# Two attentions of a fused kernel: the softmax division moved from PE transposes and DVE to a DMA round trip and GpSimd, with a new order of PE work in the causal attention's slots

## The chip, the cores and the metric

One core of a Trainium2 chip. The metric is the device time of one run in microseconds, a median over the runs shown; smaller is better.

## The reference, cut to what matters

Two layers over 16 batches of 512 tokens and 128 features. Layer 0 adds to x the output of a memory module that is trained on the sequence, and of a block made of a convolution, full attention (16 heads of size 8) and a dense mixture of 8 experts. Layer 1 adds causal attention, run twice: the second pass takes its queries from a convolution over the first pass's context, with the same keys and values. It also adds a mixture with 32 experts and top-8 routing.

```python
# layer 0
x = conv1d(x); q, k, v = split(x @ wqkv.T + bqkv)          # 16 heads of 8
ctx = softmax(q @ k.T / sqrt(8)) @ v
# layer 1
ctx = causal(q, k, v)                                      # "first" turn
q2 = conv1d(ctx) + conv_b
ctx2 = causal(q2, k, v)                                    # "second" turn
out = ctx2 @ out_w.T + out_b
```

## The kernel before

It has four stages, one after the other: `learn`, `attend0` (the attention of layer 0; tiles named `c_...`), `mixture` (`a_...`) and `layer1` (both causal attentions and the routed experts; `b_...`, `r_...`). The change touches only `attend0` and `layer1`, which share the class `Attention`.

**Turns and slots.** An attention of one batch is a turn. `attend0` has 16 turns. `layer1` has 32: `turns` mixes first passes and second passes as f0, f1, f2, s0, f3, s1 and so on. A turn has 16 slots: slot s is group g = s // 4 (four heads) and key tile t = s % 4. I call the slots t = 0 to 3 of one group a quarter. In slot s, turn p's scores for this tile are made (`tensor_scores`, L1286, and in the causal case the mask products of L1293), the exponentials are taken on ACT (`b_prob`, `c_prob`, L1401), and the product with the values of an earlier slot is added to the accumulator in bank 7 (`tensor_values`, L1317). Beside it PE makes the scores of turn p+1 in the other layout (L1254, masks L1260) for DVE to take row maxima (L1461). The maxima are transposed (L1267), split in two on DVE (L1469, L1470: `shift`) and written into turn p+1's query rows by DMA (L1232, `sync_shift`).

In the causal case the widths shrink: scores are 512, 384, 256 and 128 wide for t = 0 to 3. For t = 0 and 1 the four heads come in two units of two heads, `scores(0)` and `scores(1)`; for t = 2 and 3 they are one unit.

**Two PSUM rings set the order.** `s` has three banks of 512 columns (scores for the exponentials, convolution, queries, keys, the `whole` transposes); `m` has two pairs of banks (maxima, shift, context, values, output). PE runs its instructions in the written order. When it wants a bank that ACT or DVE has not yet freed, everything behind waits.

**The context.** An accumulation lasts two groups, a pair: two pairs a turn. After it ACT copies the accumulator to `c` (L1407, `scalar_context`, in slot 8 for pair 0 and in slot 0 of the next turn for pair 1); each head has 8 rows of sums and a ninth row, the softmax denominator. PE transposes `c` (`tensor_context`, L1327, four transposes, slots 9 and 1), DVE takes the reciprocal of the denominators and multiplies (`vector_context`, L1481, L1483), into `ctxn`. In slot 3 PE transposes both halves back (`tensor_whole`, L1335) and ACT copies them: in `attend0` to `ctxt` (L1780), which is stored to memory (L1655); in `layer1` to `cpad` for a first turn, the input of the convolution (L2894), or to `ctxt` (L2935) for a second turn, the input of the output projection (L2913).

**Other work in the turns.** In `layer1`, in the turn two ahead of a first pass: queries in slot 0 (L2885), keys in slot 4 (L2889), values in slot 8 (L2905). Two ahead of a second pass: the convolution in two halves in slots `CONVOLVE` = (4, 8). The output projection stands in slot `OUTPUT` = 5 of the turn behind a second pass. After keys or convolution GpSimd splits the queries (and keys) into three bf16 parts (`pool_parts`, L1181 to L1187), and SP spreads them to rows with 6 or 12 DMAs (`sync_rows`, L1208, L1211). SP's queue in a turn of `layer1` is, in order: `sync_shift(p, 1)`, expert weights, a load of the sums, `sync_rows(p + 2)`, a load of x (L1912), `sync_shift(p + 1, 0)` (slot 12), and the store of a result. The queue of GpSimd is: bias of a result (L2865), gathers, `pool_parts(p + 2)`, scatter-adds. Turns 0 to 8 of `layer1` also carry the routed experts.

## Time and profile before

| | |
|---|---|
| median of 3 runs | 3461.34 us (3455.52 to 3463.75) |
| the profiled execution: its time, and its span | 3481.77 us, 3480.0 us |
| mean granted TensorE clock of the profiled execution | 0.969 |
| busy share of the span | PE 92%, PE weight load 54%, DVE 74%, ACT 60%, GpSimd 24% |
| `attend0` | its context copies run from 448.8 to 1144.7 us |
| `layer1` | its context copies run from 2296.6 to 3470.4 us |

The span is the profiled execution seen by the trace; what lies around it is 1.8 us. The profiled execution took 20 us more than the median of the runs, so differences are carried over, not totals. Busy time of PE is modelled: matmuls overlap, and the start of one to the start of the next says more than a duration.

### The profile page before, as it was taken

To read this page: it belongs to the slowest core of one execution; us is meant where nothing else is said; L and a number is where in the kernel's file an instruction comes from. 1 tells how busy PE (TensorE), PEld (TensorE's weight loads), DVE (VectorE), ACT (ScalarE), POOL (GpSimd) and SP (SyncE) were. 2 spreads that over 40 slices of the span, in tenths; PEclk is the share of its full clock that TensorE was granted. 3 is DMA by queue.
4 is the path that set the end of the run, shared out by engine and by line. 5 is a ranking of instruction groups with operands and counts; after the bars stand their busy time and mean duration, and the time that the engine had idled before them with its cause. 6 is when DMAs were issued, how large, how long until landed. Compare 5 with 4: busy or idle time off the path is not lost. (4 is left out here: it accounts for less than half of the span.)

```text
span 3480.0 us, 80944 instructions
## 1 busy us (share of the span) xinstructions
PE 3216.7 (92%) x32139; PEld 1880.7 (54%) x32139; DVE 2559.9 (74%) x5088; ACT 2087.3 (60%) x4201; POOL 831.7 (24%) x756
## 2 busy tenths in 40 slices
PE   6887599999999899999999999789999999999998
PEld 5876233333333577777777777545555545444454
DVE  5876788888887376667667667677777777777774
ACT  6774188888888443434343434156667777776766
POOL 3321111111110242242242243223332211111110
PEclk8998799999999999999999999789999999999998
DMA  4100211111110001011011001222222121112110
GB/s 140 33 13 1 62 47 56 56 56 56 56 43 28 27 23 36 23 33 36 23 33 30 29 23 33 64 60 62 59 60 42 53 61 45 48 42 57 39 32 25
DMA packets 180487, 152.11 MB, mean 44 GB/s; under 512 B 44388, under 2 KB 160900, under 8 KB 179972
## 3 DMA queue, kind: packets, MB, share of 16 engines
q1 hardware_dynamic: 173092, 141.21, 14.4%
q0 software_dynamic: 6144, 4.72, 1.0%
q8 instruction: 271, 4.44, 0.5%
q10 hardware_dynamic: 864, 0.79, 0.1%
q14 instruction: 116, 0.95, 0.1%
HBM read 48.45 MB, written 32.65 MB: 23 GB/s over the span
## 5 line engine op out<-in xcount | busy, mean ns | idle before, releaser
L1461 DVE TENSOR_REDUCE b_maxima<-psum 128x2 f32<-128x1024 f32 (+3 forms) x768 | 774.4, 1045 | 239.0 <-PE psum L1260 215.3
L1401 ACT ACTIVATE b_prob<-psum 128x512 f32<-128x512 f32 (+2 forms) x1536 | 725.6, 526 | 329.0 <-PE psum L1293 299.9
L1461 DVE TENSOR_REDUCE c_maxima<-psum 128x2 f32<-128x1024 f32 x512 | 594.3, 1219 | 60.4 <-PE psum L1254 60.3
L1401 ACT ACTIVATE c_prob<-psum 128x512 f32<-128x512 f32 x1024 | 551.1, 597 | 121.6 <-PE psum L1286 101.2
L2213 PEld LDWEIGHTS psum<-consts_layer,a_hid 128*128 128x128 f32 x4096 | 476.2, 192 | 53.6 <-issue 53.3
L2203 PE MATMUL psum<-a_x1t,consts_layer 128*128 128x512 f32 x1024 | 464.0, 599 | 16.1 <-issue 10.5
L2213 PE MATMUL psum<-consts_layer,a_hid 128*128 128x128 f32 x4096 | 477.8, 274 | 0.0
L2273 ACT ACTIVATE a_hid<-psum,consts_layer 128x512 f32<-128x512 f32 x512 | 348.1, 687 | 211.0 <-PE psum L2203 205.1
L1286 PE MATMUL psum<-b_qa,b_ka 64*128 64x512 bf16 (+3 forms) x2048 | 365.5, 303 | 60.8 <-ACT b_prob L1401 56.5
L1317 PE MATMUL psum<-b_prob,b_v 128*32 128x512 f32 (+3 forms) x4096 | 387.6, 451 | 0.2
L2435 DVE SCALAR_TENSOR_TENSOR a_acc<-psum,a_gprob,a_acc 128x128 f32<-128x128 f32 x512 | 143.7, 343 | 270.4 <-PE psum L2213 258.4
L1317 PE MATMUL psum<-c_prob,c_v 128*32 128x256 f32 (+1 forms) x3840 | 320.2, 405 | 1.6 <-ACT c_prob L1401 0.6
L1254 PE MATMUL psum<-b_ka,b_qa 62*128 62x512 bf16 (+3 forms) x2048 | 300.2, 307 | 20.5 <-DVE b_maxima L1461 11.7
L2203 PEld LDWEIGHTS psum<-a_x1t,consts_layer 128*128 128x128 f32 x1024 | 188.1, 192 | 220.9 <-issue 210.9
L1286 PEld LDWEIGHTS psum<-b_qa,b_ka 64*128 64x128 bf16 x2048 | 123.2, 93 | 298.0 <-ACT b_prob L1401 221.7
L1293 PE MATMUL psum<-b_kmask,b_pick 64*128 64x64 bf16 x4096 | 253.0, 191 | 0.0
L1254 PE MATMUL psum<-c_ka,c_qa 62*128 62x512 bf16 x1024 | 202.9, 388 | 33.2 <-DVE c_maxima L1461 17.9
L1260 PE MATMUL psum<-b_qmask,b_pick 64*128 64x64 bf16 x4096 | 221.9, 191 | 2.5 <-issue 2.5
L1260 PEld LDWEIGHTS psum<-b_qmask,b_pick 64*128 64x128 bf16 x4096 | 194.7, 97 | 52.7 <-issue 5.8
L1293 PEld LDWEIGHTS psum<-b_kmask,b_pick 64*128 64x128 bf16 x4096 | 185.2, 95 | 46.9 <-issue 1.1
L1286 PE MATMUL psum<-c_qa,c_ka 64*128 64x512 bf16 x1024 | 205.9, 387 | 0.9 <-ACT c_prob L1401 0.8
L1254 PEld LDWEIGHTS psum<-b_ka,b_qa 62*128 62x128 bf16 x2048 | 106.7, 95 | 161.0 <-DVE b_maxima L1461 68.3
(406 smaller groups left out, 4286.6 us busy)
## 6 DMA issues: line engine op xcount, KB each, us to landing
b_qa<-b_part SPq DMA_DIRECT2D x192, 128.0 KB
c_qa<-c_part SPq DMA_DIRECT2D x96, 128.0 KB, 2.4
b_ka<-b_part SPq DMA_DIRECT2D x96, 128.0 KB
c_ka<-c_part SPq DMA_DIRECT2D x90, 128.0 KB, 2.4
consts_layer<-layer_in SPq DMA_DIRECT2D x1, 5419.0 KB, 19.2
c_xt<-xnt SPq DMA_DIRECT2D x17, 256.0 KB, 2.8
m_xin<-x SPq DMA_DIRECT2D x16, 256.0 KB, 4.3
xnt<-m_xt SPq DMA_DIRECT2D x16, 256.0 KB, 2.7
```

The source lines that it names most:

```text
L1254: last = nc.tensor.matmul(out[:, half, k0:k0 + w], qa[rows, hh, t * P:(t + 1) * P], ka[rows, hh, 0:w], start=True, stop=not self.causal)
L1260: last = nc.tensor.matmul(out[:, half, k1:k1 + HALF], self.pick[n][rows, :], self.qmask[rows, :], start=False, stop=n == 1)
L1286: last = nc.tensor.matmul(outs[half][:, k0:k0 + w], ka[rows, hh, t * P:(t + 1) * P], qa[rows, hh, q0:S], start=True, stop=not self.causal)
L1293: last = nc.tensor.matmul(outs[half][:, k0 + n * HALF:k0 + (n + 1) * HALF], self.pick[n][rows, :], self.kmask[rows, :], start=False, stop= ...
L1317: product = nc.tensor.matmul(self.acc[32 * j:32 * (j + 1), q0:q1], self.values(p)[:, t, column:column + 32], self.prob[:, s % 2, j, q0:q1] ...
L1401: self.nc.scalar.activation(out, src, ACT.Exp, scale=SCALE).then_inc(self.s.free, 1)
L1461: self.nc.vector.reduce_max(out, src, X).then_inc(self.m.free, 1)
L2203: nc.tensor.matmul(bank[4 + u % 3], K("up0", e * F0 + f * P, P), x1t[n][:, :], start=True, stop=True).then_inc(up_ready.sem, 1)
L2213: last = nc.tensor.matmul(tiled(2 + e % 2)[:, t, :], hid[:, e % 2, f, t * P:(t + 1) * P], K("down0", (e * FC + f) * D, D), start=f == 0, s ...
L2273: nc.scalar.activation(hid[:, e % 2, f, :], bank[4 + u % 3], ACT.Relu, bias=K("upb0", u, 1)).then_inc(hid_ready.sem, 1)
L2435: last = nc.vector.scalar_tensor_tensor(acc[n][:, t, :], tiled(2 + e % 2)[:, t, :], gprob[n][:, t, e:e + 1], acc[n][:, t, :], ALU.mult, AL ...
```

## The change

Both attentions now divide with the queries along the free axis. After ACT's copy SP issues two DMAs per pair: the eight denominator rows go from `c` to `spread` as 128 x 32 values, and all of `c` goes to `context_d` in memory. DVE takes the reciprocal of `spread` (`vector_inverse`): pair 1 in slot 3 of the next turn, pair 0 in slot 14 (15 in the causal case). SP stores it to `inverse_d`, waits until it has landed, loads it with each row repeated eight times into `scale`, and loads the contexts, with the gaps dropped, into `unscaled`. When both pairs are there GpSimd multiplies the two tiles (`normalise`) straight into `ctxt` or `cpad`. `tensor_context`, `tensor_whole`, `vector_context` and ACT's copy of the whole are gone.

In the causal attention PE's order within a slot is written out for each t: in t = 0 the work of the `m` ring stands ahead of `scores(1)`; in t = 1 the values are split in two halves around `scores(1)`; in t = 2 there are no values and they follow at the start of t = 3; in t = 3 the values of t = 2 are split in two halves. In the first slot of a pair the unsplit product now goes with the first half. `CONVOLVE` becomes (7, 9) and `OUTPUT` 10.

```diff
         self.c_copied = sig("c_copied")
+        self.spread_loaded = [sig(f"spread_loaded{n}") for n in range(PAIRS)]
+        self.inverted = sig("inverted")
+        self.inverse_stored = [sig(f"inverse_stored{n}") for n in range(PAIRS)]
+        self.scale_loaded = [sig(f"scale_loaded{n}") for n in range(PAIRS)]
+        self.normalised = sig("normalised")
+        self.context_d = nc.dram_tensor(name + "_context", [PAIRS, P, S], F32, kind="Internal").ap()
+        self.inverse_d = nc.dram_tensor(name + "_inverse", [H, S], F32, kind="Internal").ap()
 
     def late(self, ctx):
...
         self.c = [sb(f"c{n}", [P, S]) for n in range(2)]
-        self.rsum = sb("rsum", [P, T, 2 * HG])
-        self.ctxn = [sb(f"ctxn{n}", [P, T, D]) for n in range(2)]
+        self.spread = [sb(f"spread{n}", [P, S // SPREAD]) for n in range(PAIRS)]
+        self.unscaled = sb("unscaled", [P, S])
+        self.scale = sb("scale", [P, S])
 
     def has(self, p):
...
 
-    def ended(self, p, s):
-
-        jobs = [(p - 1, PAIRS - 1)] if s == 1 else [(p, s // (2 * T) - 1)] if s > 2 * T and s % (2 * T) == 1 else []
+    def inverting(self, p, s):
+
+        early, late = (3, 15) if self.causal else (3, 14)
+        jobs = [(p - 1, PAIRS - 1)] if s == early else [(p, 0)] if s == late else []
         return [job for job in jobs if self.has(job[0])]
...
                     self.m.add(*job)
-                if s == WHOLE and self.has(p - 1):
-                    self.s.add("whole", p - 1)
...
+
+        heads = slice(pair * 2 * HG, (pair + 1) * 2 * HG)
+        sp.wait_ge(self.c_copied, p * PAIRS + pair + 1)
+        if p:
+            sp.wait_ge(self.normalised, p)
+        sums = self.c[pair][DH::GAP, :].rearrange("k (b x) -> k b x", b=SPREAD)
+        sp.dma_start(self.spread[pair][:, :], sums).then_inc(self.spread_loaded[pair], 16)
+        sp.dma_start(self.context_d[pair], self.c[pair][:, :]).then_inc(self.spread_loaded[pair], 16)
+
+    def sync_inverse(self, sp, p, pair):
+
+        heads = slice(pair * 2 * HG, (pair + 1) * 2 * HG)
+        rows = slice(pair * HALF, (pair + 1) * HALF)
+        sp.wait_ge(self.inverted, p * PAIRS + pair + 1)
+        sp.dma_start(self.inverse_d[heads, :].rearrange("k (b x) -> (k b) x", b=SPREAD), self.spread[pair][:, :]
+                     ).then_inc(self.inverse_stored[pair], 16)
+        sp.wait_ge(self.inverse_stored[pair], 16 * (p + 1))
+        inverse = self.inverse_d[heads, :].unsqueeze(1).broadcast_to([2 * HG, DH, S])
+        sp.dma_start(self.scale[rows, :], inverse).then_inc(self.scale_loaded[pair], 16)
+        sp.wait_ge(self.spread_loaded[pair], 32 * (p + 1))
+        context = self.context_d[pair].rearrange("(k x) q -> k x q", x=GAP)[:, 0:DH, :]
+        sp.dma_start(self.unscaled[rows, :], context).then_inc(self.scale_loaded[pair], 16)
+
+    def normalise(self, engine, compute, p, out):
+        for pair in range(PAIRS):
+            engine.wait_ge(self.scale_loaded[pair], 32 * (p + 1))
+        compute.tensor_tensor(out, self.unscaled[:, :], self.scale[:, :], ALU.mult).then_inc(self.normalised, 1)
...
         if first and half is not None:
-            if half == 0:
+            if half == int(self.causal):
                 return
             half = None
...
 
-    def tensor_context(self, pe, p, pair):
-        out = self.m.bank("context", p, pair)
-        pe.wait_ge(self.c_copied, p * PAIRS + pair + 1)
-        pe.wait_ge(self.m.free, self.m.room("context", p, pair))
-        for t in range(T):
-            last = self.nc.tensor.transpose(out[:, 0, t * P:(t + 1) * P], self.c[pair % 2][:, t * P:(t + 1) * P], self.K("ident"))
-        last.then_inc(self.m.ready, 1)
-
-    def tensor_whole(self, pe, p):
-        out = self.s.bank("whole", p)
-        pe.wait_ge(self.m.free, self.m.count("context", p, PAIRS - 1))
-        pe.wait_ge(self.s.free, self.s.room("whole", p))
-        for t in range(T):
-            last = self.nc.tensor.transpose(out[:, t * P:(t + 1) * P], self.ctxn[p % 2][:, t, :], self.K("ident"))
-        last.then_inc(self.s.ready, 1)
-
     def tensor_turn(self, pe, p, extra_s, extra_m):
...
             def on_s():
-                if s == WHOLE and self.has(p - 1):
-                    self.tensor_whole(pe, p - 1)
                 extra_s(p, s)
...
-                scores(0)
-                maxima(0)
-                on_s()
-                scores(1)
-                on_m()
-                values(1)
-                maxima(1)
+                if t == 0:
+                    scores(0)
+                    maxima(0)
+                    on_s()
+                    on_m()
+                    scores(1)
+                    values(1)
+                    maxima(1)
+                elif t == 1:
+                    scores(0)
+                    maxima(0)
+                    on_s()
+                    values(1, 0)
+                    scores(1)
+                    on_m()
+                    values(1, 1)
+                    maxima(1)
+                elif t == 2:
+                    scores(0)
+                    maxima(0)
+                    on_m()
+                    on_s()
+                else:
+                    values(2)
+                    scores(0)
+                    maxima(0)
+                    on_s()
+                    values(1, 0)
+                    on_m()
+                    values(1, 1)
...
     def scalar_context(self, act, p, pair):
         act.wait_ge(self.pv_ready, p * SLOTS + (pair + 1) * 2 * T)
-        if p * PAIRS + pair >= 2:
-            act.wait_ge(self.m.free, self.m.count("context", *divmod(p * PAIRS + pair - 2, PAIRS)))
-        self.nc.scalar.activation(self.c[pair % 2][:, :], self.acc, ACT.Copy).then_inc(self.c_copied, 1)
+        if p:
+            act.wait_ge(self.spread_loaded[pair], 32 * p)
+        self.nc.scalar.activation(self.c[pair][:, :], self.acc, ACT.Copy).then_inc(self.c_copied, 1)
...
 
-    def vector_context(self, dve, p, pair, own):
-        nc = self.nc
-        dve.wait_ge(self.m.ready, self.m.count("context", p, pair))
-        if p * PAIRS + pair:
-            dve.wait_ge(self.m.free, self.m.count("context", *divmod(p * PAIRS + pair - 1, PAIRS)))
-        if pair == 0 and p >= 2:
-            dve.wait_ge(self.s.ready, self.s.count("whole", p - 2))
-        src = self.m.bank("context", p, pair)[:, 0, :].rearrange("p (t k x) -> p t k x", t=T, x=GAP)
-        own.done(nc.vector.reciprocal(self.rsum[:, :, :], src[:, :, :, DH]))
-        out = self.ctxn[p % 2][:, :, pair * 2 * HG * DH:(pair + 1) * 2 * HG * DH].rearrange("p t (k d) -> p t k d", d=DH)
-        nc.vector.tensor_tensor(out, src[:, :, :, 0:DH], self.rsum[:, :, :].unsqueeze(3).broadcast_to([P, T, 2 * HG, DH]), ALU.mult
-                                ).then_inc(self.m.free, 1)
+    def vector_inverse(self, dve, p, pair):
+        dve.wait_ge(self.spread_loaded[pair], 32 * (p + 1))
+        self.nc.vector.reciprocal(self.spread[pair][:, :], self.spread[pair][:, :]).then_inc(self.inverted, 1)
...
                 self.vector_shift(dve, *job, own)
-            for job in self.ended(p, s):
-                self.vector_context(dve, *job, own)
+            for job in self.inverting(p, s):
+                self.vector_inverse(dve, *job)
...
                         att.sync_shift(sp, p, 1)
+                    if att.has(p - 1):
+                        att.sync_spread(sp, p - 1, PAIRS - 1)
                     if att.has(p + 2):
                         sp.wait_ge(att.s.free, att.s.count("conv", p + 2, 1))
                         sp.dma_start(xc_d[(p + 2) * P:(p + 3) * P, :], xc[:, :]).then_inc(xc_stored, 16)
                     if att.has(p + 4):
                         load_x(p + 4)
                     if att.has(p - 1):
-                        sp.wait_ge(att.s.free, att.s.count("whole", p - 1))
+                        att.sync_inverse(sp, p - 1, PAIRS - 1)
+                        sp.wait_ge(att.normalised, p)
                         sp.dma_start(ctxt_d[(p - 1) * P:p * P, :], ctxt[:, :]).then_inc(ctxt_stored, 16)
                     if att.has(p + 2):
                         att.sync_rows(sp, p + 2)
+                    if att.has(p):
+                        att.sync_spread(sp, p, 0)
                     if att.has(p + 1):
                         att.sync_shift(sp, p + 1, 0)
+                    if att.has(p):
+                        att.sync_inverse(sp, p, 0)
                     if p == LAST - 1:
...
+                        pool.wait_ge(ctxt_stored, 16 * p)
+                    att.normalise(pool, nc.gpsimd, p, ctxt[:, :])
+
+                for p in range(-1, LAST - 1):
+                    if att.has(p - 1):
+                        normalise_context(p - 1)
+                    att.pool_parts(pool, p + 2, att.s.count("k", p + 2))
+                normalise_context(LAST - 2)
                 own = OwnSteps(ctx0, nc, "c_pool_own", pool)
                 pool.wait_ge(a.context_loaded.sem, a.context_loaded.at(0, 2))
                 nc.gpsimd.tensor_tensor(xc0[:, :], xc0[:, :], K("cols0")[:, 5:6].broadcast_to([P, S]), ALU.add).then_inc(a.xc_biased.sem, 1)
...
                 nc.gpsimd.tensor_tensor(a.acc[0][:, :, :], a.acc[0][:, :, :], over(K("ln1b"), T), ALU.add).then_inc(a.x1_ready.sem, 1)
...
             @block.tensor
             def _(pe):
...
-                        act.wait_ge(ctxt_stored, 16 * p)
-                    nc.scalar.activation(ctxt[:, :], att.s.bank("whole", p), ACT.Copy).then_inc(att.s.free, 1)
-
                 def first_batch(job):
                     if job == "z":
                         act.wait_ge(att.m.ready, att.m.count("z"))
...
+        QUERIES, KEYS, VALUES, CONVOLVE, OUTPUT = Front.QUERIES, Front.KEYS, Front.VALUES, (7, 9), 10
 
         routed = Routed(ctx, ctx0, nc, K, att, FIRST_GROUP, chosen, gate_up, down, table_d, sum_d)
...
                 for p in range(-1, len(turns) + 1):
+                    if att.has(p - 1):
+                        att.sync_spread(sp, p - 1, PAIRS - 1)
                     if att.has(p):
...
                                      ).then_inc(before_loaded, 16)
+                    if att.has(p - 1):
+                        att.sync_inverse(sp, p - 1, PAIRS - 1)
                     if att.has(p + 2):
                         att.sync_rows(sp, p + 2)
...
                         att.sync_shift(sp, p + 1, 0)
+                    if att.has(p):
+                        att.sync_spread(sp, p, 0)
+                        att.sync_inverse(sp, p, 0)
                     if p in outputs:
                         i, b = order.index(p), outputs[p].batch
...
                 for n in range(1, att.n_keys):
                     att.pool_value(pool, n)
+                def normalise_context(p):
+                    b = turns[p].batch
+                    if turns[p].first:
+                        if b >= 2:
+                            pool.wait_ge(att.s.ready, att.s.count("q", turns.index(seconds[b - 2]), 1))
+                        att.normalise(pool, nc.gpsimd, p, cpad[b % 2][:, 1:S + 1])
+                    else:
+                        if b:
+                            pool.wait_ge(att.m.ready, att.m.count("out", b - 1))
+                        att.normalise(pool, nc.gpsimd, p, ctxt[:, :])
+
                 for p in range(-1, len(turns) + 1):
+                    if att.has(p - 1):
+                        normalise_context(p - 1)
                     if p in outputs:
                         i, b = order.index(p), outputs[p].batch
...
+                        pe.wait_ge(att.s.free, att.s.room("q", p + 2, n))
+                        pe.wait_ge(att.normalised, turn_of(b) + 1)
...
-                        pe.wait_ge(att.s.free, att.s.count("whole", p - 1))
+                        pe.wait_ge(att.normalised, p)
```

## Rows read from the trace of the kernel before

**Rows 1.** Windows, a turn each: us; busy PE, PEld, DVE, ACT, POOL; clock, DMA.

```profile
785.00:830.50 45.50, 44.39 (x407) 13.93 (x408) 40.01 (x42) 38.08 (x72) 6.34 (x4) 1.00 0.18 54
3044.77:3081.07 36.30, 34.39 (x550) 17.77 (x546) 28.09 (x35) 25.38 (x54) 7.62 (x5) 1.00 0.25 68
```

**Rows 2.** Waits of 2700 to 3436 us (`layer1`): total us, times, longest.

```profile
PE psum L1286 <- ACT b_prob L1401: 40.0, 128, 0.5
```

**Rows 3.** Timeline of `attend0`: start us, us, engine, line, operation, count [idle before].

```profile
812.42 0.39 PE L1286 MATMUL psum<-c_qa,c_ka 64*128 64x512 bf16 x2
...
812.68 0.60 ACT L1407 ACTIVATE c_c<-psum 128x512 f32<-128x512 f32 x1
...
813.42 0.63 PE L1327 MATMUL psum<-consts_shared,c_c 128*128 128x128 f32 x4 [0.40 <-ACT c_c L1407]
813.98 0.39 PE L1286 MATMUL psum<-c_qa,c_ka 64*128 64x512 bf16 x2
...
815.78 0.39 PE L1286 MATMUL psum<-c_qa,c_ka 64*128 64x512 bf16 x2
...
818.03 0.39 PE L1286 MATMUL psum<-c_qa,c_ka 64*128 64x512 bf16 x2
...
822.67 9.14 DVE L1461 TENSOR_REDUCE c_maxima<-psum 128x2 f32<-128x1024 f32 x8
```

**Rows 4.** Timeline of `layer1`, PE: slots 9 to 15 of one turn.

```profile
3030.75 0.44 PE L1286 MATMUL psum<-b_qa,b_ka 64*128 64x384 bf16 x2
...
3034.36 0.27 PE L1286 MATMUL psum<-b_qa,b_ka 64*128 64x256 bf16 x2
...
3037.06 0.39 PE L1286 MATMUL psum<-b_qa,b_ka 64*128 64x512 bf16 x2
...
3038.25 0.39 PE L1286 MATMUL psum<-b_qa,b_ka 64*128 64x512 bf16 x1 [0.26 <-ACT b_prob L1401]
...
3039.49 0.32 PE L1286 MATMUL psum<-b_qa,b_ka 64*128 64x384 bf16 x2
...
3040.52 0.33 PE L1286 MATMUL psum<-b_qa,b_ka 64*128 64x384 bf16 x1 [0.26 <-ACT b_prob L1401]
...
3042.07 0.27 PE L1286 MATMUL psum<-b_qa,b_ka 64*128 64x256 bf16 x2
...
3044.77 0.39 PE L1286 MATMUL psum<-b_qa,b_ka 64*128 64x512 bf16 x2
```

**Rows 5.** Groups by line: xcount | busy us, mean ns | idle before.

```profile
L1481 DVE RECIPROCAL b_rsum<-psum 128x32 f32<-128x32 f32 x64 | 22.9, 358 | 34.8 <-PE psum L1327 33.7 <-issue 0.9
L1483 DVE TENSOR_TENSOR b_ctxn<-psum,b_rsum 128x256 f32<-128x256 f32 x64 | 27.2, 425 | 2.2
L2305 POOL TENSOR_TENSOR a_share<-a_gprob,consts_layer 128x512 f32<-128x512 f32 x120 | 125.9, 1050 | 268.9 <-DVE a_gprob L2366 260.7
```

**Rows 6.** Timeline of `layer1`, GpSimd and SP, the turn from 3044.77.

```profile
3051.77 1.28 POOL L2865 TENSOR_TENSOR b_before<-b_before,consts_layer 128x512 f32<-128x512 f32 x1 [17.64 <-DMA b_before<-sum]
3057.17 1.04 POOL L1181 CAST b_part<-b_qk 128x1024 bf16<-128x1024 f32 x1 [4.12 <-ACT b_qk L2944]
...
3063.76 0.59 SPq L1208 DMA_DIRECT2D b_qa<-b_part  x1
...
3072.31 0.60 SPq L1912 DMA_DIRECT2D b_xt<-xnt  x1
3075.89 1.12 SPq L1232 DMA_DIRECT2D b_qa<-b_shift  x2
```

**Rows 7.** DMA issues: xcount, KB each, median us from issue to landing.

```profile
ctxt<-c_ctxt SPq DMA_DIRECT2D x16, 256.0 KB, 2.0
...
b_xt<-xnt SPq DMA_DIRECT2D x16, 256.0 KB, 3.2
```

**Rows 8.** Timeline of the end of the span.

```profile
3470.40 0.60 ACT L1407 ACTIVATE b_c<-psum 128x512 f32<-128x512 f32 x1 [0.54 <-PE psum L1317]
...
3477.25 0.38 SPq L2848 DMA_DIRECT2D result<-b_res  x1
```

37 lines of the change are left out of this document (10 added, 27 removed).

## The prediction

> **What bounds the kernel now.** I read the windows of one turn of each attention first [rows 1]. In `attend0` a turn of 45.5 us has 44.4 us of PE, 40.0 of DVE and 38.1 of ACT: PE sets the pace and the two others are close behind. In `layer1` a turn of 36.3 us has 34.4 us of PE, 28.1 of DVE and 25.4 of ACT. GpSimd works for 6 to 8 us of either, so it has room. The waits of `layer1` come second [rows 2]: PE's open stalls are nearly all of one kind, scores that want a bank that ACT has not yet read: 128 times in 736 us, 40.0 us. Third I read the timeline slot by slot, because PE runs in order, and what a removed instruction is worth depends on whether it filled a stall. So three things are to be found: which transposes lay in a stall, what the new order fills, and whether the longer way by memory and GpSimd comes back in time.
>
> **First attention, the transposes.** A slot without extras lasts 2.25 us (815.78 to 818.03), and slot 9, with a context, lasts 3.36 (812.42 to 815.78) [rows 3]. The excess of 1.1 us is not what goes. ACT's copy of 0.60 us stands between its exponentials. The four transposes begin 1.00 us into the slot, after that copy, and the next scores at 1.56. Without them `scores(1)` needs the bank of the slot's first exponential: the copy starts at 0.26 and ends at 0.86, that exponential ends about 0.55 later, and PE can go on at about 1.45. Then come the maxima (0.25) and the unsplit product (about 1.0, as today), with a gap of 0.3 that stays: the slot takes 3.0. Each context gives 0.35, most of it being cover for a stall that is then bare. Slot 3 is different: `tensor_whole` is four more transposes of one kind with no copy ahead of them, and goes whole, at the 0.56 between 813.42 and 813.98. Per turn 2 x 0.35 + 0.56, about 1.2 us; by 16 turns, 19 us.
>
> DVE loses per turn two times 0.36 + 0.42 and gets two reciprocals of 128 x 32, of the same shape as today's 0.36 [rows 5]. The one in slot 3 follows the convolution of slot 2, where DVE has just been idle. The one in slot 14 lies in a stretch where DVE runs without a break, 9.14 us for 8 maxima, 1.14 each, against 1.12 for half a slot of PE. DVE has some 0.5 us before PE wants the bank, and 0.36 fits into it. I take nothing; were the cover gone it would cost 0.36 x 16 = 6 us.
>
> **Second attention, the transposes.** A quarter without extras lasts 7.71 us (3037.06 to 3044.77) with one shift transpose in it. Slot 9 lasts 3.61 us (3030.75 to 3034.36) against 2.58 (3039.49 to 3042.07) for the same slot without a context [rows 4]: 0.56 of it are transposes and the rest is ACT's copy, that delays the bank for `scores(1)`. In the new order the unsplit product (1.0 us) stands ahead of `scores(1)` and waits for the copy. From the start of the quarter: exponentials of t = 0 end at 2.73, the copy at 3.33, the product at 4.4, `scores(1)` at 4.7, and ACT, which ran dry at 4.25, starts again at 4.95; its first exponential frees the bank for t = 2 at 5.5, where PE waits 0.5. Carried on with today's distances the quarter ends at 8.15, against 8.5 to 8.6 now. A context is worth 0.4: twice 0.4 a turn. Slot 3 loses the whole: 0.56.
>
> **Second attention, the new order.** In a quarter without a context today's `scores(1)` comes 1.19 us after the slot's start in t = 0 and 1.03 in t = 1 [rows 4], about 0.55 later than without the wait. In t = 0 only `m` work can fill this: a shift transpose (0.2) in slot 12 of all turns and in slot 0 of those without queries, and the values projection (1.1 us, fills 0.55) in slot 8 of half the turns: together 0.6 to 0.5 a turn, taken as 0.5. In t = 1 half of the product fills the 0.55. A split product costs more: halves start 0.57 apart, a whole of 512 takes 0.99, so 0.15 each, and both t = 0's and t = 2's are split: 0.3 lost, 0.2 to 0.3 left over as gain at best with ACT's later start; I take 0.2 for each of two quarters, 0.4. The convolution at slot 4 covered such a stall; at slot 7 it covers none: minus 0.6 in half the turns, 0.3. At slot 9 it covers the wait for the copy instead: nothing. `OUTPUT` goes from one slot that it doesn't fill to another: nothing. Per turn 0.8 + 0.56 + 0.5 + 0.4 - 0.3, about 2.0; by 32 turns 63 us. Bounds: nothing from the order (contexts and whole at 1.0: 32 us), and all stalls gone (another 8 x 0.3 of the measured 0.31 mean: 4.4 a turn, 140 us).
>
> **What the DMA way adds.** SP gets five issues per pair at 0.4 to 0.6 each and one wait for a landing. A store of 256 KB lands 2.0 us after its issue, a load 3.2 [rows 7]; the new ones are of 16 to 256 KB, so I take 2.0 for stores and 2.4 for the loads, which are 128 KB in SBUF writes, between those rows. For pair 1, from the start T of the turn: copied 4.2; spread and context issued and landed 7.2; DVE reaches its place in slot 3 at 9.2, so no stall; inverted 9.55; stored 11.7; both loads issued by 12.5, landed 14.7; GpSimd multiplies in 1.05 [rows 5]: 15.8. Its consumers, the output projection at slot 10 and the convolution at slot 7, come later.
>
> But this multiplication stands in GpSimd's queue ahead of the bias of a result and of `pool_parts`. In a turn with keys the parts start today at T + 12.4 (3057.17) and end at 19.0 [rows 6]. Behind the multiplication and the bias (1.28) they start at 17.1 and end at 23.7; SP's twelve row DMAs and the load of x take 9.1 (3063.76 to 3072.9), to 32.8; only then `sync_shift(p + 1, 0)` issues (1.12, today at T + 31.1 when its data is ready) and lands at about 35.4. PE wants it at slot 0 of the next turn, at about 36.3 - 2.4 = 33.9. It is 1.5 us late, in the turns with keys; I take 1.2. In turns with a convolution the parts come 2.5 us later than now, because slot 9 replaces 8; the shift still lands in time, with some 0.3 to spare, but `sync_spread(p, 0)` behind it lands 1 us after DVE wants it in slot 15, and DVE holds the maxima of the next turn for 0.5. Turns with routed experts are longer and I count 4 us for all nine. Sum: 11 x 1.2 + 11 x 0.5 + 4, 23 us. Bounds: 0, if loads land at 2.0 and the rows are issued at 0.59 each, and 60.
>
> The Trainium skill, "DMA: Bandwidth & Descriptors", section "Anatomy of one DMA", puts nearly all of a transfer's fixed 2.0 us into the receipt of the write and calls memory the slowest target, so a load into SBUF should land no later than a store. The trace says the reverse here (3.2 against 2.0) [rows 7]. By the page the two loads would land at some 14.3 and the lateness would be 0.4 us a turn less: estimated by the page, the sum would be 4 us lower.
>
> **The two ends.** Today the last copy starts at 3470.40 and the result's store at 3477.25, 6.9 us [rows 8]. In the new chain: copy 0.6, spread 0.4 + 0.4 + 2.0, reciprocal 0.4, store 2.1, loads 0.9 + 2.4, multiplication 1.1, then projection and addition as now, 3.5: 13.8, so 7 us more. `attend0` ends in the same way with all engines waiting for it; DVE's own work there hides a part: 5 us. Bounds 2 and 10 each.
>
> **Sum.** -19 - 63 + 23 + 7 + 5 = -47 us on the profiled 3482, to 3435. The median of the runs lies 20 us below the profiled execution; I carry that distance over: 3461.3 - 47 = 3414.
>
> **The rivals.** (a) The transposes and bank stalls count almost in full: 2 us a turn in `attend0`, 3.5 in `layer1`, and no lateness. For it: PE is busy 98% of a turn of `attend0` [rows 1]. Against it: the copy on ACT stays, and it alone delays the bank. -32 - 112 + 12 = -132: 3330; half-way forms lie at 3350 to 3380.
>
> (b) The new order brings nothing, since the product ahead of `scores(1)` starves ACT as much as it spares PE. For it: ACT dry for 0.7 us in my own schedule. 32 turns at 1.0 give 32; with 19, 23 and 12: -16, 3445.
>
> (c) Slower: the way reciprocal, store, load, multiplication, parts, rows, shift becomes the length of a turn. Its three memory landings, each later by x, add 3x to each turn with keys (15) and about 2x to the others once their 0.3 of slack is gone. It decides from 15 x 3x + 15 x 2x = 47, so from x = 0.6 us. At x = 1.2 it gives +45: 3505. For it: loads at 3.2 in the same queue [rows 7], and 128-byte pieces, which this trace doesn't show in these places. Against it: the DMA engines are 18 to 25% busy [rows 1]. The Trainium skill, "DMA: Bandwidth & Descriptors", section "Specifications", says that pieces under 512 bytes are written by read-modify-write; no run here shows its price yet.
>
> **How the numbers follow.** Forecast (3390 to 3440) 0.50; (a) with its half-way forms 0.20; (b) with weaker lateness or gain, 3440 to 3465, 0.15; (c) 0.15. A measurement here tells 0.2%, 7 us, from no change. Of (b) a third, and a bit of (c), lie within 7 us: same 0.07. Of (c) 0.13 is slower. Faster: 0.80. The range 3360 to 3465 leaves out the far half of (a) and most of (c). The likeliest case's own range is 3390 to 3440.
>
> **What would show it.** `attend0`'s turn at 44.3 us instead of 45.5; slot 9 at 3.0; slot 3 at 2.25. In `layer1` the wait of L1286 for ACT smaller in t = 1, and new waits of L1317 for `b_c` in slots 1 and 9. On SP `sync_shift(p + 1, 0)` issued right behind the rows in turns with keys, and at slot 0 PE idle for a DMA into `b_qa`. DVE idle before a reciprocal in slot 15. GpSimd's multiplication at T + 15, about 1.05 us. Wrong would make it: PE idle for `b_qa` for more than 3 us a turn, a multiplication well over 1.3 us, or DVE waiting in slot 3.

## The result and the profile after

The changed kernel takes 3436.13 us (median of 4 runs, 3434.5 to 3448.47) against 3460.95 us (4 runs) of the kernel before measured beside it: ratio 0.9938, interval 0.9912 to 0.9964. The ratio compares means and stands for 21 us, its interval for 12 to 30; the medians lie 25 us apart, since one of the four runs, the profiled one, took 12 us more than the others. The forecast was 47 us. The profiled execution took 3448.47 us, its span is 3446.4.

**The turns, by windows.** One turn of `attend0`, one of `layer1` with keys, the one with a convolution ahead of it, and most of the turns without experts. Columns as in [rows 1].

```profile
783.98:828.18 44.20, 42.77 (x402) 12.70 (x394) 39.13 (x40) 37.23 (x71) 7.55 (x5) 1.00 0.26 81
3012.40:3047.67 35.27, 31.30 (x570) 17.08 (x568) 27.06 (x32) 24.13 (x52) 8.78 (x6) 1.00 0.32 88
2977.00:3012.40 35.40, 34.39 (x579) 18.62 (x576) 25.87 (x30) 24.74 (x53) 4.83 (x5) 0.90 0.22 65
2720.00:3380.00 660.00, 606.08 (x10682) 330.63 (x10682) 488.33 (x573) 451.80 (x960) 124.93 (x104) 0.96 0.27 78
```

`attend0` came out as forecast: 44.2 us a turn (44.3 predicted), PE still busy for all but 1.4 us of it. In `layer1` PE has gaps now: 31.3 of 35.3 us. And the granted clock, 1.00 in the turn of [rows 1], is 0.90 in one of these turns and 0.96 over 660 us.

**The waits of the turns without experts** (2615 to 3397 us), PE's and DVE's. Compare [rows 2].

```profile
PE psum L1322 <- DMA b_qa<-b_shift: 25.8, 9, 4.1
PE psum L1322 <- ACT b_prob L1440: 16.5, 66, 0.3
PE psum L1290 <- DVE b_maxima L1498: 8.9, 12, 1.8
PE psum L1353 <- ACT b_c L1446: 7.9, 18, 0.5
...
DVE b_spread L1512 <- DMA b_context<-b_c: 54.6, 28, 5.1
```

The order did what it says: PE waits 16.5 us for `b_prob`, and 42.3 in the same turns of the kernel before. But a new line stands above it: nine times PE stands for the shift, 2.9 us each. And DVE stands 28 times for a reciprocal's input, 54.6 us.

**The chain of one turn with keys**, which follows the forecast's own chain. Its slot 0 starts at T = 3011.43 on PE. The timeline of SP, GpSimd, PE and DVE:

```profile
3016.04 0.61 SPq L1240 DMA_DIRECT2D b_spread<-b_c  x1
...
3020.74 0.33 SPq L1248 DMA_DIRECT2D b_inverse<-b_spread  x1
...
3022.16 0.62 SPq L1252 DMA_DIRECT2D b_scale<-b_inverse  x1
...
3022.83 0.60 SPq L1255 DMA_DIRECT2D b_unscaled<-b_context  x1
...
3026.32 1.28 POOL L1260 TENSOR_TENSOR b_ctxt<-b_unscaled,b_scale 128x512 f32<-128x512 f32 x1 [22.45 <-DMA b_unscaled<-b_context]
...
3033.20 2.12 POOL L1194 TENSOR_TENSOR b_part<-b_rest,b_part 128x1024 bf16<-128x1024 f32 x1
...
3035.35 0.60 SPq L1215 DMA_DIRECT2D b_qa<-b_part  x1
...
3044.61 1.18 SPq L1268 DMA_DIRECT2D b_qa<-b_shift  x2
3045.89 0.65 SPq L1240 DMA_DIRECT2D b_spread<-b_c  x1
...
3047.67 0.39 PE L1322 MATMUL psum<-b_qa,b_ka 64*128 64x512 bf16 x2 [2.38 <-DMA b_qa<-b_shift]
...
3048.78 0.35 DVE L1512 RECIPROCAL b_spread<-b_spread 128x32 f32<-128x32 f32 x1 [3.32 <-DMA b_context<-b_c]
```

Counted from T, with the forecast in brackets: inverse issued 9.3 (9.55); its store landed when SP issues the next DMA, 10.7 (11.7); product starts 14.9 (14.7) and ends 16.2 (15.8); parts end 23.9 (23.7); rows from there to 32.5, shift issued 33.2 (32.8), PE goes on at 36.2 (landed 35.4). PE wanted it at 33.9 (33.9). So each step of the chain is within a microsecond, and the stall is 2.4 us instead of 1.5. What the forecast did not follow in such a turn is the line behind the shift and the last one: the denominators of pair 0 are issued at 3045.89, and DVE stands 3.3 us for them.

This is one of the milder turns; the nine stalls are 1.2 to 4.1 us long. In the worst (T = 2792.76, stall 4.1 us) the store of the inverse took 2.9 us to land and the product started at T + 17.0, 2.1 us later than here; in that of T = 3082.89 (3.9 us) the load of `unscaled` took 4.4 us to land. The worst:

```profile
2802.52 0.33 SPq L1248 DMA_DIRECT2D b_inverse<-b_spread  x1
...
2805.38 0.64 SPq L1252 DMA_DIRECT2D b_scale<-b_inverse  x1
...
2809.74 1.27 POOL L1260 TENSOR_TENSOR b_ctxt<-b_unscaled,b_scale 128x512 f32<-128x512 f32 x1 [26.36 <-DMA b_unscaled<-b_context]
```

**The end of the span**, the timeline from the last copy on; compare [rows 8]:

```profile
3428.77 0.60 ACT L1446 ACTIVATE b_c<-psum 128x512 f32<-128x512 f32 x1 [0.55 <-PE psum L1353]
...
3442.50 0.39 SPq L2894 DMA_DIRECT2D result<-b_res  x1
```

13.7 us (13.8 forecast) instead of 6.9.

### The profile page after: what moved, and what is told of

Read it like the earlier page. It is cut to its first block and busy times, and to the rows that moved or that the text cites. A ratio compares the mean times of both kernels' runs of the same rounds, so it can differ in the third digit from the quotient of the medians.

```text
span 3446.4 us, 83138 instructions
## 1 busy us (share of the span) xinstructions
PE 3143.0 (91%) x33099; PEld 1862.0 (54%) x33099; DVE 2512.0 (73%) x4992; ACT 2060.3 (60%) x4153; POOL 891.7 (26%) x804
## 5 line engine op out<-in xcount | busy, mean ns | idle before, releaser
L1498 DVE TENSOR_REDUCE b_maxima<-psum 128x2 f32<-128x1024 f32 (+3 forms) x768 | 780.2, 1043 | 222.0 <-PE psum L1296 213.8
L2312 ACT ACTIVATE a_hid<-psum,consts_layer 128x512 f32<-128x512 f32 x512 | 347.1, 687 | 212.4 <-PE psum L2242 205.4
L1353 PE MATMUL psum<-b_prob,b_v 128*32 128x128 f32 (+3 forms) x5632 | 409.0, 379 | 10.3 <-ACT b_c L1446 9.7
L1322 PE MATMUL psum<-b_qa,b_ka 64*128 64x512 bf16 (+3 forms) x2048 | 347.4, 309 | 53.1 <-DMA b_qa<-b_shift 28.1
L1290 PE MATMUL psum<-b_ka,b_qa 62*128 62x512 bf16 (+3 forms) x2048 | 310.2, 311 | 35.7 <-DVE b_maxima L1498 26.1
L1329 PE MATMUL psum<-b_kmask,b_pick 64*128 64x64 bf16 x4096 | 243.8, 192 | 0.0
L1322 PE MATMUL psum<-c_qa,c_ka 64*128 64x512 bf16 x1024 | 218.1, 387 | 19.3 <-ACT c_prob L1440 18.9
L1296 PEld LDWEIGHTS psum<-b_qmask,b_pick 64*128 64x128 bf16 x4096 | 202.8, 98 | 54.6 <-issue 11.0
L2344 POOL TENSOR_TENSOR a_share<-a_gprob,consts_layer 128x512 f32<-128x512 f32 x120 | 125.8, 1048 | 267.1 <-DVE a_gprob L2405 258.8
```

Of the source, the lines that this page charges most:

```text
L1290: last = nc.tensor.matmul(out[:, half, k0:k0 + w], qa[rows, hh, t * P:(t + 1) * P], ka[rows, hh, 0:w], start=True, stop=not self.causal)
L1296: last = nc.tensor.matmul(out[:, half, k1:k1 + HALF], self.pick[n][rows, :], self.qmask[rows, :], start=False, stop=n == 1)
L1322: last = nc.tensor.matmul(outs[half][:, k0:k0 + w], ka[rows, hh, t * P:(t + 1) * P], qa[rows, hh, q0:S], start=True, stop=not self.causal)
L1329: last = nc.tensor.matmul(outs[half][:, k0 + n * HALF:k0 + (n + 1) * HALF], self.pick[n][rows, :], self.kmask[rows, :], start=False, stop= ...
L1353: product = nc.tensor.matmul(self.acc[32 * j:32 * (j + 1), q0:q1], self.values(p)[:, t, column:column + 32], self.prob[:, s % 2, j, q0:q1] ...
L1498: self.nc.vector.reduce_max(out, src, X).then_inc(self.m.free, 1)
```

## The experiments

Some readings compare stages. Their boundaries are the starts of DVE's second shift operation on 16 x 128 (L1470 before, L1507 after; slot 0 of each turn): 16 of them in `attend0`, 32 in `layer1`. The first nine distances in `layer1` are the turns with experts, the last 22 those without, which I call plain. Plain turns alternate between two kinds: with a convolution and with keys. Their lengths are means of the first nine of each kind; the last turns differ, since the work ahead of them ends. Time at 1.2 GHz is summed from the granted clock of windows of 1 us.

### First group, on one chip: the halves of the change, and two of its waits

The kernel before took 3461.38 us there (12 runs).

**path_only**: the DMA way without the new order and slots.

```diff
-        QUERIES, KEYS, VALUES, CONVOLVE, OUTPUT = ..., (7, 9), 10
+        QUERIES, KEYS, VALUES, CONVOLVE, OUTPUT = ..., (4, 8), 5
         # and tensor_turn, tensor_values as before
```

> The changed kernel with the old order of PE's work in the causal attention and the old slots of the convolution and the output (4, 8 and 5). Theory 1 (the way by memory and the order each gain, and both are eaten where a turn has no routed experts because the shift and the spread land late): the first attention keeps its 1.3 us a turn; in the second the contexts and the whole give 1.4 us a turn, the turns with keys are still late by about 2 us; 20 us below the kernel before, 3440. Theory 2 (the new order costs as much as it spares, and the gain in the turns with experts is the removed transposes): 35 us below, 3426, so better than the changed kernel.

3497.0 us, ratio 1.0103 (1.0087 to 1.0118). That is slower than before, where both theories had a gain (3440 and 3426). PE's waits in the plain turns:

```profile
PE psum L1322 <- ACT b_prob L1417: 42.4, 135, 0.5
PE psum L2950 <- POOL b_ctxt L1260: 39.4, 11, 5.4
PE psum L2931 <- POOL b_cpad L1260: 8.1, 1, 8.1
```

L2950 is the output projection. In slot 5 it comes before GpSimd's product, 3.6 us each time. Here the plain turns take 812.7 us, 32 more than before, and these stalls alone are more than that. The move of `OUTPUT` to slot 10, which the forecast priced at nothing, takes them away: without it the DMA way loses.

**order_only**: the kernel before with the new order and the new slots.

> The kernel before with the new order of PE's work and the new slots (7, 9 and 10) only; transposes and DVE's division stay. Theory 1: about 0.6 us a turn of the second attention, more in the turns with experts, 20 us below the kernel before, 3440; turns without experts at 35.0 in place of 35.5. Theory 2: within 7 us of the kernel before.

3451.33 us, ratio 0.9974 (0.9963 to 0.9984). The plain turns take 777.4 us in all instead of 780.2: 0.1 us a turn, where the first theory had 0.6. The kernel gains 9 us, half of what it said; the rest of that must lie in other turns, which no profile of the kernel before shows for this group. PE's waits in the plain turns:

```profile
PE psum L1317 <- ACT b_c L1430: 14.1, 32, 0.5
PE psum L1254 <- DVE b_ctxn L1506: 10.9, 44, 0.2
PE psum L1286 <- ACT b_prob L1424: 6.6, 26, 0.3
```

The stalls for `b_prob` are nearly gone (42.3 us in the same turns of the kernel before), and two others have come. That for `b_ctxn`, the old division on DVE, goes with the DMA way. That for ACT's copy `b_c` stays: 14.0 us, 32 times, in both_mended too.

**parts_first**: the change, but in turns with keys GpSimd makes the parts before it multiplies.

```diff
                 for p in range(-1, len(turns) + 1):
+                    if first(p + 2):
+                        att.pool_parts(pool, p + 2, att.s.count("k", p + 2))
                     if att.has(p - 1):
                         normalise_context(p - 1)
...
-                    if att.has(p + 2):
-                        att.pool_parts(pool, p + 2, ...)
+                    if second(p + 2):
+                        att.pool_parts(pool, p + 2, att.s.count("q", p + 2, 1))
```

> The changed kernel, but in turns with keys GpSimd makes the parts of queries and keys before it multiplies the context. Theory 1: PE's wait for the shift rows at slot 0 (28 us in all) goes nearly whole, and DVE's wait for the spread in slot 15 (79 us in all) shrinks by half; turns with keys fall from about 37 to 35 us; 15 to 25 us below the changed kernel, 3415. Theory 2: under 5 us, since PE is busy anyway and the waits only move.

3400.32 us, ratio 0.9818 (0.9805 to 0.9831). The plain turns take 742.8 us, against 781.6 in the changed kernel: 39 us, more than either theory had. PE's wait for the shift is gone; of DVE's wait 20 us are left:

```profile
PE psum L1322 <- ACT b_prob L1440: 17.5, 70, 0.3
...
DVE b_spread L1512 <- DMA b_context<-b_c: 20.3, 21, 3.1
```

**spread_apart**: the change, with the denominators of pair 0 issued ahead of the shift (in turns with a convolution ahead of the rows), and a semaphore of their own, so that DVE does not wait for the 256 KB store of `c`.

```diff
+                    if att.has(p) and not first(p + 2):
+                        att.sync_spread(sp, p, 0)
                     if att.has(p + 2):
                         att.sync_rows(sp, p + 2)
...
+                    if att.has(p) and first(p + 2):
+                        att.sync_spread(sp, p, 0)
                     if att.has(p + 1):
                         att.sync_shift(sp, p + 1, 0)
                     if att.has(p):
-                        att.sync_spread(sp, p, 0)
                         att.sync_inverse(sp, p, 0)
```

> The changed kernel, but SP issues the spread of pair 0 ahead of the shift (ahead of the rows too in turns with a convolution), and DVE waits for the spread alone, not for the store of the contexts. Theory 1: DVE's wait before the reciprocal falls from 79 us to under 15; PE's wait for the shift grows by 1 us a turn with keys, as two more issues stand ahead of it; 10 to 20 us below the changed kernel, 3420. Theory 2: under 5 us.

3435.86 us, ratio 0.9925 (0.9911 to 0.9938): nothing clear of the noise against the changed kernel (0.9938), as the second theory has it. The waits of the plain turns say why (one of DVE's ten, 6.2 us, lies behind them, at the end of the span):

```profile
PE psum L1323 <- DMA b_qa<-b_shift: 34.6, 9, 5.2
...
DVE b_spread L1514 <- DMA b_spread<-b_c: 24.6, 10, 6.2
```

The turns with a convolution fell to 33.2 to 34.6 us, but those with keys rose to 38: the two DMAs ahead of the shift make it later by 1 us. The wait went from DVE to PE.

### Second group, on another chip: both waits mended, and the order under it

The kernel before took 3481.98 us there (9 runs).

**both_mended**: the edits of parts_first and spread_apart together.

> The changed kernel with both mends: the parts ahead of the multiplication in turns with keys, and the spread of pair 0 issued ahead of the shift with DVE waiting for the spread alone. Theory 1 (lateness at the turn's head is all that the changed kernel loses): the last DVE wait of 24 us goes too, turns of the second attention without experts at 33.3 us, 10 us below parts_first, 3390. Theory 2 (DVE's wait is cover: PE is the bound and has half a microsecond in hand): equal to parts_first within 5 us, as spread_apart was to the changed kernel.

3431.89 us, ratio 0.9856 (0.9842 to 0.9869). Plain turns 33.1 and 33.8 us, 734.5 us in all: 2.1 us a turn less than before, as forecast for a kernel without lateness. The gain over the kernel before is 50 us, not the 70 that the forecast has without its term for lateness: the turns with experts take 387.5 us, and 388.2 in before_again. Against parts_first the total says nothing, since that was measured in another group; both_again below settles it.

**order_undone**: both_mended with the old order and `CONVOLVE` = (4, 8), `OUTPUT` still 10.

> As both_mended, but PE's order within the causal slots and the slots of the convolution (4, 8) as in the kernel before; the output projection stays at slot 10. Theory 1: the order is worth what order_only showed in the turns without experts, 0.1 us a turn, and 2 in those with: 20 us above both_mended, 3410. Theory 2: the order is worth more once the transposes are gone, since nothing is left that fills the stall of the scores: 40 us above, 3430.

3457.8 us, ratio 0.9929 (0.9916 to 0.9943). That is 26 us above both_mended, between the two theories (20 and 40). Plain turns 754.3 us, so the order is worth 19.8 us in them. But it is not spread evenly: 8.0 us lie in the last turn but one, with a single stall of 6.9 us, and 2.2 in the last. In the twenty turns ahead of them the order is worth 9.8 us, 0.5 a turn:

```profile
PE psum L1323 <- ACT b_prob L1418: 43.1, 135, 0.5
PE psum L2938 <- POOL b_cpad L1261: 6.9, 1, 6.9
```

**scores_ahead**: both_mended with the unsplit product behind `scores(1)`.

```diff
     def tensor_values(self, pe, p, s, half=None):
...
         if first and half is not None:
-            if half == int(self.causal):
+            if half == 0:
                 return
```

> As both_mended, but in the first slot of a pair the unsplit product stands behind the second scores again. Theory 1 (the product ahead of the scores waits for ACT's copy and then starves ACT): 0.3 us less in two slots a turn, 15 us below both_mended. Theory 2 (the scores' own wait for a bank costs as much): within 7 us of it.

3428.62 us, ratio 0.9847 (0.9833 to 0.9860), plain turns 733.6 us: the same as both_mended, as the second theory has it.

**before_again**: the kernel before, profiled a second time.

> The kernel before, unchanged, for a second profile. The first profile took 20 us more than the runs and that of order_only none. Theory 1: the second profile lies within 8 us of the runs, and the turns with experts are then near 40 us, not 43; so a part of the gain that the profiles show in those turns is none. Theory 2: the profile is again 3480 and the turns are as in the first.

3488.27 us profiled. Plain turns 780.2 us, to the tenth as in the first profile; turns with experts 388.2 us (384.6): it lies 6 us above the median of the runs beside it, as the first theory has it, but the turns with experts take 43 us each, as the second does.

### Third group, one chip: where the gain sits, stage by stage

The kernel before took 3487.06 us there (9 runs). **before_third**, **after_again**, **parts_again** and **both_again** are kernels already shown, profiled on one chip.

> The changed kernel once more, unchanged, on one chip with the two mended versions and a profile of the kernel before. Open is where its 21 us come from: its turns without experts gain nothing (34.9 with a convolution, 37.0 with keys, before 35.3 and 35.8), attend0 gives 15 and its end takes 5, the end of the span takes 8. Theory: ratio 0.993 to 0.995, and the nine turns with experts are some 18 us shorter in sum than those of the kernel before on this chip, since they have slack for the late landings and gain 2 us each. Rival: the turns with experts gain nothing and the distance is another between kernels: then their sums agree within 5 us.

> parts_first once more, on one chip with both_mended. Theory (its gain against the kernel before was 61 us on one chip, both_mended's 50 us on another, and the difference is the chip's): ratio 0.985 to 0.989 here, turns without experts 33.2 and 35. Rival: the kernel itself is better than both_mended in the turns with experts, and the ratio is again near 0.982.

> both_mended once more. Theory: turns without experts of 33.1 and 33.8, 22 x 0.5 = 10 us less than parts_first in them, so 5 to 12 us faster than parts_again on the same chip: ratio 0.983 to 0.986. Rival: the second change (the early denominators and a semaphore of their own) costs in the turns with experts what it gives in the others: equal to parts_again or slower, with a sum of the nine turns with experts 10 us or more above parts_again's.

> The kernel before, unchanged, for a profile on the same chip as the three others. Theory: turns without experts 35.3 and 35.8 as in both profiles so far; the nine turns with experts vary with the chip (384.6 and 388.3 us in the two profiles so far), and on a chip where the kernel takes 3461 us their sum is some 20 us lower. Rival: their sum is the same here, and the 20 us between the profiled execution and the median lie in another stage.

The theories for parts_again and both_again hold in the ratio. That for after_again misses: 0.9957, and 7 us in the turns with experts, between its 18 and the rival's none. That for before_third stays open, since the kernel takes 3487 us here and not 3461.

| us | before_third | after_again | parts_again | both_again |
|---|---|---|---|---|
| ratio (interval) | | 0.9957 (0.9944 to 0.9971) | 0.9853 (0.9838 to 0.9869) | 0.9838 (0.9824 to 0.9851) |
| up to `attend0`'s first boundary | 421.9 | 427.3 | 426.9 | 426.6 |
| `attend0`, 15 distances | 673.7 | 655.2 | 655.5 | 655.5 |
| to `layer1`'s first boundary | 1173.9 | 1179.9 | 1180.3 | 1181.1 |
| nine turns with experts | 391.2 | 384.4 | 383.8 | 387.9 |
| 22 plain turns | 780.2 | 781.5 | 739.7 | 734.5 |
| to the end of the span | 42.0 | 46.7 | 46.6 | 46.3 |
| span | 3483.0 | 3475.0 | 3432.7 | 3431.9 |
| at 1.2 GHz in the plain turns | 0.0 | 58.0 | 3.4 | 0.0 |

The first row of stages is no effect of the change: the kernel before shows 425.0, 427.9 and 421.9 in its three profiles. For the rest, the changed kernel gains 18.5 us in `attend0`, gives back 6 at its end and 5 at the end of the span, gains 7 in the turns with experts, and gains nothing at all in the 22 turns where the forecast saw 25. Mended, the same turns gain 45.7. The second mend is worth 5 us in the plain turns (739.7 to 734.5) and as much between the medians, but the intervals of the two ratios overlap.

The turns with experts gain 7 us in the changed kernel and 3 in both_again; 14 were forecast, and 18 without lateness. In the changed kernel's first profile and in the first group their sums are lower: 352.3 (changed kernel) and 350.9 (parts_first), both 32 to 33 us less than here, and 363.2 (order_only). The kernel before is 20 to 26 us faster there too. So the groups differ in these turns, and a kernel's ratio moves with that (parts_first 0.9818, parts_again 0.9853): more than its interval says. Whether the chip is the cause is not shown; the first and the fourth group even carry the same chip number. Totals are therefore compared within a group, and between groups only the plain turns, which the kernel before (780.2 three times) and the changed one (781.6 and 781.5) repeat.

### Fourth group, one chip: the stall or the clock behind it

The kernel before took 3480.93 us there (13 runs). The windows had shown a second thing beside each late shift. PE stands, and behind the stall the granted clock is at the 1.2 GHz level for a while. Windows of the changed kernel, behind the stalls that ended at 2756.21 and 3047.67 us:

```profile
2756.00:2760.00 4.00, 3.77 (x41) 1.64 (x43) 2.12 (x5) 2.63 (x5) 0.00 (x0) 0.50 0.22 73
...
3048.00:3052.00 4.00, 3.90 (x49) 1.82 (x47) 2.86 (x5) 3.16 (x7) 0.00 (x0) 0.58 0.10 30
```

Time at 1.2 GHz is 54.6 us in the plain turns of the changed kernel and nothing before: up to 27 us, if PE alone set the pace. It comes in ten stretches, eight of them with a stall for the shift and two with a stall of 1.7 to 1.8 us for DVE's maxima; none came with the shortest stall for the shift (1.2 us).

**after_filled**: the changed kernel, with eight useless 128 x 128 products ahead of the wait, in the nine plain turns where the shift is late.

```diff
     def tensor_scores(self, pe, p, s, u):
+        if self.causal and s == 0 and u == 0 and p > 9 and self.has(p + 1) and self.turns[p + 1].first:
+            pe.wait_ge(self.s.free, ...)
+            for _ in range(8):
+                nc.tensor.matmul(bank[:, 0:P], self.K("ident"), self.K("ident"), start=True, stop=True)
         if t == 0 and u == 0 and g in (0, EARLY):
             pe.wait_ge(self.shift_loaded[0 if g == 0 else 1], 32 * (p + 1))
```

> The changed kernel with eight useless 128 x 128 products on PE ahead of the wait for the late shift, in the nine turns without experts in which it is late. They keep PE busy while it would stand; nothing lands earlier. Theory (half of the lateness is the clock that falls behind the stall): no stretch at 1.2 GHz in these turns, granted clock 1.00 there instead of 0.96, and the 22 turns without experts take 755 to 765 us instead of 781.5; ratio 0.987 to 0.991. Rival (the stall costs its own length): the fill changes nothing or adds its excess, 781 to 790 us.

3459.43 us, ratio 0.9936 (0.9919 to 0.9953). Plain turns 778.4 us, 20.5 us of them at 1.2 GHz: neither the theory's 755 to 765 nor the rival's 781 to 790. PE's waits there:

```profile
PE psum L1328 <- ACT b_prob L1446: 17.5, 70, 0.3
PE psum L1291 <- DVE b_maxima L1504: 16.1, 19, 2.1
PE psum L1328 <- DMA b_qa<-b_shift: 10.4, 6, 2.7
```

**both_filled**: both_mended with the same products.

> both_mended with the same eight products in the same nine turns, where no stall stands. It prices the fill: eight products at 0.27 us are 2.2 us a turn, 9 x 2.2 = 20 us at most on 734.5 for the turns without experts, less what ACT's and DVE's buffers hide. Theory: 745 to 755 us, clock 1.00. Rival for the reading of after_filled: if the fill costs nothing here, then PE has room and the two kernels differ by more than the clock.

3445.32 us, ratio 0.9898 (0.9882 to 0.9915). Plain turns 752.8 us instead of 734.5; those with keys 35.8 instead of 33.8, the others unchanged: the fill costs 2.03 us each time and PE has no room for it. No time at 1.2 GHz. All of this is as its theory has it.

Together: the fill takes the place of 18 us of the wait, 10 are left, 28.7 in all against 25.8 unfilled. 34 us at 1.2 GHz went, and the turns got 3 us shorter, 6 when the longer sum of waits is allowed for. The theory asked for 17 to 26. It fell: on the average of these turns a microsecond at 1.2 GHz costs about 0.2 us. A part of the reason is in the waits: PE, back at full speed, stands for DVE's maxima for 16.1 us (8.9 in the changed kernel), and DVE for the denominators for 60.4 (54.6).

The price is not the same in all turns. In spread_apart neither engine has a late input in the turns with a convolution, and the clock is what is left: they take 33.2 us with no time at 1.2 GHz and 34.2 to 34.6 with 3.4 us, and a line through ten of them has 0.4 us for each microsecond. In the changed kernel 25.6 of the 54.6 us lie in turns with a convolution. At 0.2 throughout the clock is worth some 10 us, at 0.4 in those turns some 15; both are estimates.

**before_late**: the kernel before, with six small stores on SP ahead of the shift's two DMAs in the same nine turns.

```diff
     def sync_shift(self, sp, p, n):
...
+            for k in range(6):
+                sp.dma_start(self.late_d[p, k], self.pick[0][:, 0:16]).then_inc(self.late_stored, 16)
         for w in range(2):
```

> The kernel before with six small stores (4 KB each) issued by SP ahead of the shift's two DMAs in the same nine turns, so that the shift lands some 3 us later and PE stands about 2.5 us for it. Theory: the granted clock falls behind each stall here too, 30 to 60 us at 1.2 GHz, and the nine turns cost 4 to 5.5 us each: 36 to 50 us, ratio 1.010 to 1.014. Rival (the stall costs its length, or less where ACT and DVE catch up): 10 to 23 us, ratio 1.003 to 1.007, and a clock of 1.00.

3485.03 us, ratio 1.0008 (0.9998 to 1.0018): it decides nothing, because the stall did not come about. The six issues took 2.7 to 3.5 us together, and yet PE stood for the shift only 4 times, under 1 us each:

```profile
PE psum L1292 <- DMA b_qa<-b_shift: 2.4, 4, 0.9
```

It shows another thing: the kernel before had some 2.5 to 3 us of slack on the shift (an estimate from these issues and waits). Two of them go by the turn with keys being 2 us shorter (35.8 to 33.8), and the later parts take the rest and 2.9 us more. Whether a stall alone brings the clock down in the kernel before stays untested.

## Why the prediction was right in sign and wrong in size

**Transposes of `attend0`: right.** 18.5 us over 15 distances, 1.23 a turn (1.2). The slot with the copy lasts 2.97 us (825.64 to 828.61 in the timeline; 3.0), DVE's reciprocal in slot 14 costs nothing that the turns show, and the end of the stage costs 6.0 (5).

**Transposes and order in `layer1`: right as a sum.** 2.08 us a turn in both_again (2.0, in turns of both kinds). So are its parts, outside the last two turns: the transposes alone 31.5 us over twenty turns, 1.6 a turn (1.36), then the order 0.5 (0.6 with the convolution's loss). Over all 22 turns they are 25.9 and 19.8 us, because with the old order one stall of 6.9 us stands near the end. The order without the DMA way is worth 0.1 a turn: the parts are not additive, and each was argued as if it were. `OUTPUT` was put at nothing: on the new path the old slot has 39.4 us of stalls (path_only), and on the old path no run moves it alone.

**Lateness: this step failed.** The sum has 23 us for it, 18.7 of them in the 22 plain turns (11 x 1.2 and 11 x 0.5). The runs give 781.5 - 734.5 = 47 us. The cause was named and the mechanism is shown: parts_first takes 39 to 42 us of the 47 away by moving the product behind the parts, both_mended the rest. Three things were sized wrong in it:

- The stall itself: 1.2 us was taken, for eleven turns, where the forecast's own chain had 1.5; it is 2.9 on the average of nine turns, 26 us. In the turn shown the shift was issued 0.4 us later than counted and landed another 0.4 later. In the worst turns single landings of the chain took 1 to 1.5 us more than in this one.
- What stands behind the late shift in the same queue. `sync_spread(p, 0)` follows it, and the forecast counted DVE's wait in the turns with a convolution only, at 0.5. DVE stands 54.6 us in all. Where PE stands anyway this is hidden (a turn with keys takes 33.8 us plus PE's stall, 37.0), but in the turns with a convolution it is not: 34.9 instead of 33.1.
- The clock behind the stall: not in the forecast, some 10 to 15 us in all.

How the last two share the 16 us of the turns with a convolution (nine times 1.8) is an estimate. The nine turns have 24.5 us at 1.2 GHz, some 10 us at spread_apart's 0.4; and PE waits 4.8 us in them for maxima that DVE makes late.

**Turns with experts: too high, cause open.** 14 us were forecast, 7 measured in the third group; with both waits mended 3, where the forecast without lateness has 18. They are also the turns in which the groups differ by some 30 us. The kernel before shows 20.5 to 35.3 us at 1.2 GHz there, the changed one 17.6 and 44.7 in its two profiles, both_mended 48.5. No run took this apart.

**The end: right.** 6.9 us more from the last copy to the store (7).

The terms, corrected by the one that failed: -47 + 28 = -19, against 21 measured. That the two agree is partly luck: in the third group, where the stages can be compared, they add up to -13 (and 15 by the ratio), since the turns with experts gain less as well. The result lies in the range, and in the likeliest case's own (3390 to 3440), by its upper edge; that is owed to the width of the range, the sum being off by 22 to 26 us. Of the rivals, (c) had the mechanism, a late shift by way of the parts, in a milder form than it asked for; it did not decide the sign, because the loads were 3.5 us and the small store 1.4 in most turns, where it asked for all three to be late. (Its sum at x = 1.2 is +43 us, not +45.) Rival (b), a new order that brings nothing, has almost the measured size (16 us), but not the mechanism: the order brings 0.5 us a turn in order_undone.

**Landings.** In the turn shown the load of `unscaled` lands 3.5 us after its issue (2.4 taken), the 16 KB store of the inverse 1.4 (2.1 taken), so the two errors nearly cancel; in other turns the store takes up to 3.1 us and the load over 4. The Trainium skill, "DMA: Bandwidth & Descriptors", section "Anatomy of one DMA", would have the load land no later than a store. It describes transfers issued by GpSimd, and these are issued by SyncE. The trace agrees with it only in part: of the 256 KB transfers in the changed kernel, `ctxt`'s store lands after 2.0 us and `b_xt`'s load after 3.0, but the store of a result after 3.4. Section "Specifications" of the same page has pieces under 512 bytes written by read-modify-write; the store of the inverse consists of 128-byte pieces and landed first of all, so no price of it shows here.

GpSimd's product takes 1.27 to 1.28 us (1.05 taken, from another product; the addition of the same shape in [rows 6] had taken 1.28 already).

## What to carry to other kernels

When work is moved to an engine or a queue with room, price not the operation but its place in line: list all that stands behind it, follow it to the next engine that needs it, and then list what stands behind that one too. Here an engine busy for a quarter of the time cost some 40 us through the order of two jobs in its queue; swapping them in the changed kernel gives a version at 0.9853, and with the denominators ahead of the shift as well 0.9838. When an order was made for a new path, test it with the path: alone it showed 0.1 us a turn, under the path 0.5.

## What the runs showed of the hardware that was not expected

- In a stage of otherwise unbroken work eight of nine stalls of PE for one input, 1.4 to 4.1 us long, came with a stretch at 1.2 GHz (54.6 us in 782 together with two shorter stalls for another engine, none in both_mended); products without use in the wait cut this to 20.5 us. The price was 0.2 us for each microsecond on average and 0.4 in turns in which no other engine was late (an estimate from after_filled and spread_apart).
- One stage differs between groups of runs and the others agree: the nine turns with experts take 347.1 to 365.5 us in the four kernels of the first group and 383.6 to 395.3 us in all kernels of the three others, while the 22 plain turns of the kernel before read 780.2 us in all three of its profiles. Two of these groups carry the same chip number, so the cause is open.
